# Score maxima of an attention block: one full-array matmul pair per step, or two 64-row tiles for two units in every odd step

## The reference, cut to what matters

```python
q = (x @ Wq.T).reshape(b, t, N_HEADS, HEAD_DIM)      # 8 heads of 64
kv_latent = x @ Wkv_down.T                           # rank 64
k = (kv_latent @ Wk_up.T).reshape(b, t, N_HEADS, HEAD_DIM)
scores = jnp.einsum('bqhd,bkhd->bhqk', q, k) * scale
attn = jax.nn.softmax(scores, axis=-1)
out = jnp.einsum('bhqk,bkhd->bqhd', attn, v)
```

## Time and profile before

| | us |
|---|---|
| median of 3 runs | 3176.31 (3176.28 to 3179.29) |
| the profiled execution | 3175.94 |
| its span from first to last instruction | 3174.1 |
| TensorE matmul busy | 3115.8 (98%) |
| GpSimd busy | 2556.5 (81%) |
| VectorE busy | 2295.4 (72%) |
| ScalarE busy | 1729.6 (54%) |

### The profile page before, as it was taken

How to read it: one execution, slowest core, us unless ns; L and a number is a source line. 1 busy time by engine, 2 the same in 40 slices (tenths; PEclk the granted TensorE clock), 3 DMA queues, 4 the chain that set the end, 5 groups by cost and what they waited for, 6 DMA issues and landing times.

```text
span 3174.1 us, 44918 instructions
## 1 busy us (share of the span) xinstructions
PE 3115.8 (98%) x15394; PEld 1907.2 (60%) x15394; DVE 2295.4 (72%) x2466; ACT 1729.6 (54%) x3209; POOL 2556.5 (81%) x1521
## 2 busy tenths in 40 slices
PE   6999999999999999999999999999999999999997
PEld 5556656556665665656566565666656656565555
DVE  5667777776777777777777777767777777776764
ACT  3555555555555555555555555555555555555543
POOL 2888787888878888787887878888788887887886
PEclk8999999999999999999999999999999999999998
DMA  2111111111111111111111111111111111111111
GB/s 83 41 44 58 49 53 44 52 60 44 55 54 58 48 41 58 48 64 48 44 61 44 57 45 48 64 44 54 51 61 46 43 57 48 61 44 38 55 44 40
DMA packets 161250, 162.89 MB, mean 51 GB/s; under 512 B 58112, under 2 KB 109440, under 8 KB 161024
## 3 DMA queue, kind: packets, MB, share of 16 engines
q1 hardware_dynamic: 161024, 160.03, 15.4%
HBM read 74.40 MB, written 17.33 MB: 29 GB/s over the span
## 4 chain that ended last, share of the span: by engine, by line
PE 88%; DVE 4%; issue 3%; ACT 2%; POOL 2%; DMA 1%; SPq 0%; POOLq 0%; ACTq 0%; DVEq 0%
PE ps_mix L601 26%; PE ps_score L622 15%; PE ps_max L647 14%; PE ps_score L624 13%; PE ps_side L587 7%; PE ps_side L713 4%; PE ps_side L732 3%; PE ps_side L699 2%; POOL prob_sum L987 2%; DVE neg_max L1138 1%; ACT probs L818 1%; PE ps_side L720 1%; PE ps_side L689 1%; PE ps_side L665 1%; DVE mixed L1106 1%
## 5 line engine op out<-in xcount | busy, mean ns | idle before, releaser
L987 POOL TENSOR_TENSOR prob_sum<-prob_sum,probs 128x1024 f32<-128x1024 f32 x768 | 1890.5, 2462 | 317.1 <-ACT probs L818 242.8
L1138 DVE TENSOR_REDUCE neg_max<-ps_max 128x1 f32<-128x1024 f32 x1024 | 1238.0, 1218 | 420.6 <-PE ps_max L647 411.5
L818 ACT ACTIVATE probs<-ps_score 128x512 f32<-128x512 f32 x2048 | 1112.5, 596 | 548.5 <-PE ps_score L624 537.7
L601 PE MATMUL ps_mix<-probs,values 128*64 128x512 f32 x4096 | 935.4, 598 | 0.8 <-ACT probs L818 0.8
L622 PE MATMUL ps_score<-query,key_hi 128*128 128x512 f32 x2048 | 877.3, 428 | 9.3 <-DVE query L1176 6.1
L624 PE MATMUL ps_score<-query_m,key_lo 128*128 128x512 f32 x2048 | 806.1, 394 | 0.0
L647 PE MATMUL ps_max<-key_hi,query 128*128 128x512 f32 x2048 | 642.6, 395 | 11.9 <-DVE neg_max L1138 11.5
L601 PEld LDWEIGHTS ps_mix<-probs,values 128*64 128x64 f32 x4096 | 271.3, 136 | 531.0 <-issue 529.8
L622 PEld LDWEIGHTS ps_score<-query,key_hi 128*128 128x128 f32 x2048 | 384.1, 188 | 255.1 <-ACT probs L818 102.3
L647 PEld LDWEIGHTS ps_max<-key_hi,query 128*128 128x128 f32 x2048 | 380.9, 188 | 112.2 <-DVE neg_max L1138 20.8
L987 POOL TENSOR_TENSOR prob_sum<-probs 128x1024 f32<-128x1024 f32 x128 | 319.3, 2495 | 129.2 <-ACT probs L818 129.2
(11 more groups left out here) (200 smaller groups left out, 2833.8 us busy)
## 6 DMA issues: line engine op xcount, KB each, us to landing
query_m<-query SPq DMA_DIRECT2D x128, 512.0 KB, 3.2
recip<-recip_scratch SPq DMA_DIRECT2D x254, 128.0 KB, 2.9
x_in<-in_L_attn_x_dram SPq DMA_DIRECT2D x32, 512.0 KB, 4.6
x_mid<-in_L_attn_x_dram SPq DMA_DIRECT2D x64, 256.0 KB, 3.7
out_dram<-x_mid SPq DMA_DIRECT2D x64, 256.0 KB, 2.2
denoms<-recip SPq DMA_DIRECT2D x508, 1.0 KB, 1.7
gates<-gates_scratch SPq DMA_DIRECT2D x16, 256.0 KB, 4.3
query_m<-max_row SPq DMA_DIRECT2D x128, 4.0 KB
```

What stands on the lines that cost most here:

```text
L601: last = nc.tensor.matmul(ps_mix[j * R:j * R + R, :], values[par][:, k, :], probs[:, (STEPS * z.c + s) % RING, j * HALF:(j + 1) * HALF], s ...
L818: nc.scalar.activation(probs[:, (STEPS * z.c + s) % RING, half * HALF:(half + 1) * HALF], ps_score[half], ACT.Exp, scale=SCALE).then_inc(e ...
L987: nc.gpsimd.tensor_tensor(out=total[:, :], in0=before, in1=probs[:, now % RING, :], op=ALU.add).then_inc(adds_done, 1)
L1138: nc.vector.tensor_reduce(neg_max[:, m:m + 1], ps_max[m % 2][:, :], AX_X, ALU.max, negate=True).then_inc(maxima_done, 1)
```

## The change

The maxima are computed from the high parts of the queries alone, over 64 rows. Odd heads now keep the high part on partitions 64 to 127 and the low part on 0 to 63. In each odd step four matmuls do two units, one of each head of the pair: for each half of the keys one matmul on rows 0 to 63 into `ps_max[0]` and one on rows 64 to 127 into `ps_max[1]`. Even steps have no maxima. VectorE does two reductions in an odd step, and the next pair of units waits for both. The copy into `query_m`, which keeps its old layout, becomes three DMAs.

```diff
--- before.py
+++ after.py
@@ -185,11 +185,14 @@
                 count += len(range(z.rooms().index(room), len(z.pieces), len(z.rooms())))
         return count
 
-    def max_item(self, s):
-
-        if s >= MAX_LAG:
-            return (self.n, s - MAX_LAG) if self.has_n else None
-        return (self.c, STEPS - MAX_LAG + s) if self.has_c else None
+    def max_pair(self, s):
+
+
+        if s % 2 == 0:
+            return None
+        if s > MAX_LAG:
+            return (self.n, s - 1 - MAX_LAG) if self.has_n else None
+        return (self.c, STEPS - MAX_LAG + s - 1) if self.has_c else None
 
 
 @lru_cache(None)
@@ -514,11 +517,14 @@
                         if s == copy % STEPS and there:
                             need_alone(sp, scores_ready, 2 * NT * (GROUPS * b + j - 1))
                             drained(sp, flagged(b if PLAN["query"][j] >= STEPS else b - 1), "query", j, need_alone)
-                            sp.dma_start(query_m[:, j % 2, :].rearrange("p (h n) -> p h n", h=2).bitcast(F32),
-                                         group_queries(j).bitcast(F32)).then_inc(query_m_copied, 16)
+                            even, odd = (group_queries(j)[:, h, :].bitcast(F32) for h in range(2))
+                            to = query_m[:, j % 2, :].rearrange("p (h n) -> p h n", h=2).bitcast(F32)
+                            sp.dma_start(to[:, 0, :], even).then_inc(query_m_copied, 16)
+                            sp.dma_start(to[0:R, 1, :], odd[R:P]).then_inc(query_m_copied, 16)
+                            sp.dma_start(to[R:P, 1, :], odd[0:R]).then_inc(query_m_copied, 16)
                         if s == row % STEPS and there:
                             drained(sp, z, "max_row", j, need_alone)
-                            need_alone(sp, query_m_copied, 16 * (GROUPS * b + j + 1))
+                            need_alone(sp, query_m_copied, 48 * (GROUPS * b + j + 1))
 
                             need_alone(sp, max_row_set, 16 * (GROUPS * b + j))
                             sp.dma_start(query_m[P - 1:P, j % 2, :].bitcast(F32),
@@ -627,12 +633,12 @@
 
             def maximum(z, s):
 
-                item = z.max_item(s)
+                item = z.max_pair(s)
                 if item:
                     b, m = item
                     gm, unit = divmod(m, NT)
-                    hm, qt = 2 * (gm // 2) + unit // 4, 4 * (gm % 2) + unit % 4
-                    kpar = (1 - z.par) if s >= MAX_LAG else z.par
+                    p, qt = gm // 2, 4 * (gm % 2) + unit // 2
+                    kpar = (1 - z.par) if s > MAX_LAG else z.par
                     if m % NT == 0:
 
                         drained(pe, flagged(b if PLAN["query"][gm] >= STEPS else b - 1), "query", gm)
@@ -641,13 +647,16 @@
                             pe.wait_ge(mod_kept, 2)
                         for i in range(2):
                             drained(pe, flagged(b - 1), "latent", i)
-                    need(pe, maxima_done, STEPS * b + m - 1)
-                    bank = ps_max[m % 2]
+                    need(pe, maxima_done, STEPS * b + m)
+
+
                     for half in range(2):
-                        last = nc.tensor.matmul(bank[:, half * HALF:(half + 1) * HALF],
-                                                query[:, hm, qt * P:(qt + 1) * P],
-                                                key_hi[kpar][:, half * HALF:(half + 1) * HALF],
-                                                start=True, stop=True)
+                        for j in range(2):
+                            rows = slice(j * R, (j + 1) * R)
+                            last = nc.tensor.matmul(ps_max[j][:, half * HALF:(half + 1) * HALF],
+                                                    query[rows, 2 * p + j, qt * P:(qt + 1) * P],
+                                                    key_hi[kpar][rows, half * HALF:(half + 1) * HALF],
+                                                    start=True, stop=True)
                     last.then_inc(max_scores_ready, 1)
 
             def side_work(z, s):
@@ -861,7 +870,7 @@
                             need(act, side_full[room], count + 1)
                             p, half = divmod(i, 2)
                             for j in range(2):
-                                nc.scalar.activation(query[0:R, 2 * p + j, half * HALF:(half + 1) * HALF],
+                                nc.scalar.activation(query[j * R:(j + 1) * R, 2 * p + j, half * HALF:(half + 1) * HALF],
                                                      side[j * R:(j + 1) * R, :], ACT.Copy).then_inc(query_hi_done, 1)
                         elif kind == "latent":
                             need(act, side_full[room], count + 1)
@@ -1131,11 +1140,15 @@
 
             def slot(z):
                 for s in range(STEPS):
-                    item = z.max_item(s)
+                    item = z.max_pair(s)
                     if item:
                         b, m = item
-                        need(dve, max_scores_ready, STEPS * b + m + 1)
-                        nc.vector.tensor_reduce(neg_max[:, m:m + 1], ps_max[m % 2][:, :], AX_X, ALU.max, negate=True).then_inc(maxima_done, 1)
+                        need(dve, max_scores_ready, (STEPS * b + m) // 2 + 1)
+                        gm, unit = divmod(m, NT)
+                        for j in range(2):
+                            col = NT * gm + 4 * j + unit // 2
+                            nc.vector.tensor_reduce(neg_max[:, col:col + 1], ps_max[j][:, :], AX_X, ALU.max,
+                                                    negate=True).then_inc(maxima_done, 1)
                     divide(z, s)
                     divide_last(z, s)
                     if s == FFN_LO[z.has_c] and z.has_o:
@@ -1173,8 +1186,10 @@
                             p, half = divmod(i, 2)
                             cols = slice(half * HALF, (half + 1) * HALF)
                             for j in range(2):
-                                last = nc.vector.tensor_tensor(query[R:P, 2 * p + j, cols], side[j * R:(j + 1) * R, :],
-                                                               query[0:R, 2 * p + j, cols].bitcast(F32), ALU.subtract)
+                                last = nc.vector.tensor_tensor(query[(1 - j) * R:(2 - j) * R, 2 * p + j, cols],
+                                                               side[j * R:(j + 1) * R, :],
+                                                               query[j * R:(j + 1) * R, 2 * p + j, cols].bitcast(F32),
+                                                               ALU.subtract)
                             last.then_inc(side_drained[room], 1)
                         elif kind == "latent":
                             need(dve, key_hi_done, 4 * b + 2 * (i + 1))
```

## The result

The changed kernel takes 3193.38 us (median of 5 runs, 3187.88 to 3194.98) against 3179.29 (5 runs): a ratio of 1.0042, 95% interval 1.003 to 1.0054. It is slower by 0.4%, where 1% faster was forecast. The time lies within the stated range, on the wrong side. The profiled execution took 3187.88 us, span 3186.1; it is the fastest of the five. Its span is 12.0 us over that of before, where the medians differ by 14.1.

What follows compares the result with a forecast made beforehand. TensorE was taken as the bound. Per slot, 13.0 us gained less 3.4 (odd steps), 5.4 (VectorE), 1.1 (GpSimd) and 1.0 (`norm2_t`) gave 2.1, over 16 slots 34 us: 3142 us, range 3080 to 3235.

Steps and rivals of the forecast that it cites:

- I take 0.09 each way for row tiles: TensorE's odd steps: going into or out of row tiles costs 0.09 us each way, bounds 0 and 0.19.
- What it pays in odd steps: TensorE's shape changes per slot: 1.4 us in steps 1 modulo 4, 2.0 in steps 3 modulo 4, together 3.4.
- a switch wider by 0.07 per group: Shape changes around a group of four matmuls: 0.07 us more than assumed per group would decide between gain and loss.
- The credit of 1.0: Ten even query steps per slot no longer restart slowly after a floor-bound step: 10 x 0.10 = 1.0 us gained.
- Overlap of the couples: Two row-tile matmuls run side by side: 0.23 us per couple, 0.46 if none; the no-overlap rival, 3297 us, had chance 0.11.
- the floor of 1.47: The loop score, exponential, next score takes at least 1.47 us in any step, however little TensorE does.
- VectorE: 5.4 forecast: Later groups waiting for two reductions: 5.4 us per slot, including 2.0 in steps 21 to 25 and 1.7 in 53 to 57.
- GpSimd and ScalarE: 2.1 forecast: Waits per slot: 1.1 us for GpSimd's sums at steps 41 and 49, 1.0 for the `norm2_t` drain (three times 0.35).
- the margin of 0.67: Step 41: GpSimd's last add ends 0.67 us before L699 needs it; TensorE gaining 1.6 would make it wait 0.9.
- Nothing gained: Rival: waits on VectorE and GpSimd spread to other cycles and eat the 2.1 us per slot; 3175 us, chance 0.08.
- Loads not behind their own matmul: Rival: a row tile's weights do not load behind its own matmul, 0.1 us for each couple; 3219 us, chance 0.18.
- couples 0.3 or more apart: Profile sign of exposed weight loads: a group's couples start 0.3 us or more apart, where the forecast had 0.23.

Runs made afterwards that it cites:

- Run 7: The kernel before, still one unit per step, but each as two 64-row matmuls in one row tile with nothing beside it: 3472.5 us, 1.093 of before.
- Run 1: The changed kernel with the two units of an odd step on the full 128 rows, one after the other, instead of row tiles: 3273.4 us, 1.0303 of before.
- 11: The kernel of Run 6 with its groups on the full array instead of row tiles: 3251.4 us, 1.0238 of the kernel before.
- Run 6: The changed kernel with VectorE's second reduction of an odd step moved behind that step's splits and statistics: 3158.2 us, 0.9939 of the kernel before.
- run 8: The changed kernel's units regrouped per four steps: a row-tile couple beside the mixes, one full-array unit in each of the next two steps, then none: 3231.5 us, 1.0172 of before.

## Why the prediction was wrong

**The step that failed** is "I take 0.09 each way for row tiles" (What it pays in odd steps). This term was half of what it is. Run 7 measures 0.39 for a way in and out together, 0.2 each, at the very end of the stated bound of 0.19. The row that shows the missing half was in front of me: L622 behind the 32-column tiles lasts 0.50 where others last 0.39. I measured the switch from start to start and stopped at the first matmul; the other half of the cost lies in that matmul's own duration. Per slot it makes 3.4 in place of 1.4 in steps 1 modulo 4 and 4.4 in place of 2.0 in steps 3: 4.4 us more, 70 us over 16 slots, twice the whole forecast gain of 34. With it the sum gives a loss of 2.3 us per slot in place of a gain of 2.1, so this term alone turns the sign. The prediction had said that a switch wider by 0.07 per group decides; it is wider by 0.14 (4.4 / 32).

**The credit of 1.0** for query steps that no longer restart slowly did not come. They follow a group now, and begin with the same unloaded weights: 2.43 us, not 2.31. Run 1, without tiles, has the 2.31.

**Overlap of the couples** was right, the 0.46 saved per group too (runs 1, 7 and 11), and the floor of 1.47 held in steps 2, 6, 58 and 60 to 0.04 (1.46 to 1.51).

**VectorE: 5.4 forecast, 3.6 measured, and half of it not where I looked.** I had replayed VectorE for the next maxima alone. The waits at steps 13, 17 and 25 came (0.4, 0.3, 0.9), step 57's did not, and the other 2.0 were something else: the side pieces of steps 14, 38 and 54 (1.2, 0.35, 0.5) wait for splits that stand behind two reductions. I had named what is queued behind each wait on TensorE, not what is queued behind the added reduction on VectorE. Run 6 shows it for steps 14 and 38, not for 54: the order of that one reduction is worth some 35 us in the changed kernel and 68 in run 8.

**GpSimd and ScalarE: 2.1 forecast, some 0.7 measured in the middle slots.** Step 41 took 5.82, with no wait: from step 34 to step 40 TensorE gained 0.4 us, not the 1.6 that I had reckoned, so the margin of 0.67 held. GpSimd's wait came at step 9 instead, 0.4 us, which the prediction did not have. `norm2_t` cost 0.1 each in steps 20, 36 and 52.

**The sum.** 13.0 - 3.4 - 5.4 - 1.1 - 1.0 = 2.1 became, with 4.4 more for the switches, 1.0 less credit, 0.4 less gain in the long even steps (0.44 each, not 0.46), and 3.7 less for the waits, 0.0. (A wait of 0.5 at step 24 that the kernel before had is counted against the waits.) So the time stayed near the forecast by luck: waits forecast too high hid most of a switch forecast too low. The two end slots added 12.7 us of loss, which no step of mine held; a switch of 0.09 and the order of run 6 would have shrunk them (run 6 has 3.6 and 1.8 there; the smaller switch was not run). The clock's fall in the last of them, 1.7 us, is in no term either.

**The rivals.** "Nothing gained" had the middle slots' sum right, but not its reason, since the waits were smaller than forecast. "Loads not behind their own matmul" had the right size (0.1) and the right direction, at the wrong place. Its sign, couples 0.3 or more apart, did come: they start 0.33 apart. But that is one bare load, the first couple's, and not one for each couple. The second couple's loads do run ahead: all four loads begin within 0.12 us of the first (1082.40 + 0.30 less a load of 0.18), while the first couple streams. Within such a run of matmuls only the first after a change of shape has its load bare. The Trainium skill's rule that a load overlaps a running matmul only where row groups differ ("TensorE: Matmul & The Clock Gate", Part 3, The mechanism) does not hold in these traces: the second couple's loads go to the same rows as the running first couple. The Trainium skill's page "TensorEngine Tiling (Array Packing)", Key Properties, says that a change of tiling mode drains TensorE; the trace agrees, and puts 0.2 us to each change, of which 0.1 is the load that did not go ahead.

## What to carry to other kernels

A change of tile shape has two halves: the gap before the first matmul, and the longer first matmul itself; measure to the second start. Row tiles of 64 pay where a stream saved (0.23 us per couple here) is more than the way in and out, so they belong next to work in another shape, where one way is paid already (here the mixes), or, by the same sum and not tried here, in longer groups. And when an operation is moved or doubled on an in-order engine, list everything that is queued behind it and who waits for that, not only who waits for the operation; then slots at the ends of a loop, which lack part of the cover, have to be summed apart.

## What the hardware showed that I had not expected

The change of tile shape costs 0.39 us per way in and out, with one stream of 512 columns at 0.23. Couples of the fast format overlap nearly fully: four matmuls in 0.73, like two. A split of the same size on VectorE lasted from 1.2 to 2.95 us, by where in the step it fell, and this decided whether TensorE waited.

Waits can also cost clock. In the run with the mixes first, the granted clock of the whole span fell to 0.959 from 0.995, while TensorE waited over 250 us for VectorE and GpSimd. It was at its lower level for 284 us, against 32 in the changed kernel. At that level the mixes took twice as long, so by an estimate from these numbers up to half of the 252 us between them, 126 us, of that run's 291 us over the changed kernel lie there; how much was hidden by waits was not taken apart.
